# Filler matmuls and tile-by-tile waits on TensorE in the edge loop of the last layer of a four-layer graph network

## What is computed

```python
def _L3_gnn_ref(x, edge_index, W, b):
    loops = jnp.arange(N)
    src = jnp.concatenate([edge_index[0], loops])
    dst = jnp.concatenate([edge_index[1], loops])
    deg = jax.ops.segment_sum(jnp.ones_like(dst), dst, num_segments=N)
    dinv = jax.lax.rsqrt(deg)
    norm = dinv[src] * dinv[dst]
    xw = jnp.matmul(x, W)
    msg = xw[src] * norm[:, None]
    agg = jax.ops.segment_sum(msg, dst, num_segments=N)
    return jax.nn.relu(agg + b)
...
h = jnp.maximum(_layernorm(x), 0.0)
x = x + _L3_gnn_ref(h, edge_index, L3_gnn_W, L3_gnn_b)
return x
```

## Time and profile before

| | us |
|---|---|
| median of 3 runs | 5710.36 |
| lowest and highest | 5703.56, 5723.24 |
| the profiled execution | 5696.5 |
| its span, first to last instruction | 5694.7 |
| mean granted TensorE clock in it | 0.742 |

### The profile page before, as it was taken

The page is one execution under the profiler, slowest core; times in us unless marked ns, Lnnn a source line. Parts: engine busy times, 40 slices in busy tenths (PEclk is TensorE's granted clock), DMA queues, the critical chain, the costliest instruction groups (busy, mean ns, idle before and its releaser), DMA issues. The chain is left out here.

```text
span 5694.7 us, 67915 instructions
## 1 busy us (share of the span) xinstructions
PE 3575.8 (63%) x13714; PEld 2586.3 (45%) x13714; DVE 3362.4 (59%) x9604; ACT 2025.6 (36%) x5849; POOL 3194.3 (56%) x3425
## 2 busy tenths in 40 slices
PE   8666666666699555666656477777777443444444
PEld 5444444444474444544444345555545333333333
DVE  7577777777753556666656456666666443444434
ACT  2455555555463322322222355555655200000000
POOL 1466655555300366666666466666666466666665
PEclk9776777767799777777877667767776676767777
DMA  3343333333310243333333233333333233333332
GB/s 107 90 115 111 110 107 107 107 110 111 91 38 2 84 115 105 106 104 105 104 101 105 60 92 95 96 96 97 96 95 96 63 97 98 97 97 100 96 98 84
DMA packets 345412, 539.66 MB, mean 95 GB/s; under 512 B 75657, under 2 KB 237484, under 8 KB 345036
## 3 DMA queue, kind: packets, MB, share of 16 engines
q0 software_dynamic: 146080, 385.23, 24.4%
q1 hardware_dynamic: 191467, 142.70, 8.9%
q10 hardware_dynamic: 7488, 7.72, 0.4%
HBM read 505.27 MB, written 30.07 MB: 94 GB/s over the span
## 5 line engine op out<-in xcount | busy, mean ns | idle before, releaser
L761 POOL DMA_INDIRECT e_rows<-table,src_idx x2490 | 2356.4, 946 | 1650.5 <-issue 631.3
L853 DVE TENSOR_TENSOR acc<-acc,banks 128x273 f32 (+3 forms) x3320 | 1294.5, 390 | 1392.8 <-DMA prep<-in_prep 555.4
L842 PE MATMUL banks<-e_rows,e_hot 128*128 128x128 f32 (+1 forms) x3320 | 853.2, 409 | 705.7 <-issue 415.5
L842 PEld LDWEIGHTS banks<-e_rows,e_hot 128*128 128x128 f32 x3320 | 704.9, 248 | 847.2 <-issue 692.2
L761 POOL DMA_INDIRECT edge_rows<-table,src_idx x830 | 787.8, 949 | 536.6 <-PE banks L842 210.3
L842 PE MATMUL banks<-edge_rows,e_hot 128*128 128x273 f32 x1660 | 738.7, 577 | 15.2 <-DVE edge_rows L1301 8.2
L842 PE MATMUL banks<-e_rows,e_weighted_hot 128*128 128x257 f32 x1660 | 692.9, 557 | 19.0 <-issue 14.6
L970 ACT ACTIVATE e_apart<-const,dst_loc 128x128 bf16<-128x128 f32 x1664 | 505.7, 388 | 15.9 <-PEq L539 9.1
L842 PEld LDWEIGHTS banks<-e_rows,e_weighted_hot 128*128 128x128 f32 x1660 | 401.0, 269 | 105.2 <-issue 30.5
L842 PEld LDWEIGHTS banks<-edge_rows,e_hot 128*128 128x128 f32 x1660 | 393.9, 269 | 113.2 <-DVE acc L853 15.7
L1583 PE MATMUL banks<-e_wr,e_scaledT 99*128 99x384 f32 (+1 forms) x832 | 278.2, 491 | 105.8 <-ACT e_scaledT L1505 56.1
(11 more groups left out here) (359 smaller groups left out, 5283.5 us busy)
## 6 DMA issues: line engine op xcount, KB each, us to landing
e_edge_in<-in_edge_attr SPq DMA_DIRECT2D x830, 80.0 KB
e_rows<-table,src_idx POOLq DMA_INDIRECT x2490
e_node_rows<-node_line SPq DMA_DIRECT2D x104, 256.0 KB
edge_rows<-table,src_idx POOLq DMA_INDIRECT x830
table<-n_row SPq DMA_DIRECT2D x49, 132.0 KB, 1.7
X<-in_x SPq DMA_DIRECT2D x1, 6272.0 KB
values<-table SPq DMA_DIRECT2D x49, 128.0 KB, 2.0
table<-fn_row ACTq DMA_DIRECT2D x48, 129.0 KB
```

The source lines that it names most:

```text
L761: nc.gpsimd.indirect_dma_start(out=rows[:, u, q, 0:width], out_offset=None, in_=table, in_offset=bass.IndirectOffsetOnAxis(ap=at, axis=0)) ...
L842: ins = nc.tensor.matmul(sums.area(t), onehot, rows, start=True, stop=True)
L853: nc.vector.tensor_tensor(at, at, sums.area(j * G + q), ALU.add).then_inc(added, 1)
```

## The change

It acts in the plain loop alone.

- The gathers of a batch raise 8 semaphores in place of one: `gathered` has `RING * G` = 32 entries there, indexed `u * G + q`, and `tile_arrived(n, q)` gives the count to wait for.
- TensorE no longer waits for all 8 gathers ahead of tile 0. `sum_tile` gets `arrival`, and waits for the one tile's rows right ahead of its matmul. The waits for `hot_ready` (ahead of tile 0) and `added` (ahead of each even tile) stay where they were, and come first.
- Between the wait for `added` and the wait for the rows, TensorE multiplies `ones` (128 x 128) with columns of `const` into the tile's own PSUM area: 512 columns, as two matmuls of 256, ahead of the first tile of a pair, 256 columns, one matmul, ahead of the second. The real matmul, with `start=True`, then overwrites the area. This is 3 filler matmuls for 2 real ones, all of 256 columns.

```diff
@@ gather_batches
-                                                 in_offset=bass.IndirectOffsetOnAxis(ap=at, axis=0)).then_inc(gathered[u], 16)
+                                                 in_offset=bass.IndirectOffsetOnAxis(ap=at, axis=0)).then_inc(gathered[u * G + q if tile_by_tile else u], 16)
 
             turns(gather)
             for u in range(RING):
-                pool.wait_ge(gathered[u], arrived(BATCHES - RING + u, u))
+                if not tile_by_tile:
+                    pool.wait_ge(gathered[u], arrived(BATCHES - RING + u, u))
+                for q in range(G if tile_by_tile else 0):
+                    pool.wait_ge(gathered[u * G + q], tile_arrived(BATCHES - RING + u, q))
...
+        def tile_arrived(n, q):
+
+            return 16 * sum(is_step(m, q) for m in range(n % RING, n + 1, RING))
...
-        def sum_tile(pe, j, q, onehot, rows, summed_tile, added, sums):
+        def sum_tile(pe, j, q, onehot, rows, summed_tile, added, sums, arrival=None):
 
             if not is_step(j, q):
                 return
             t = j * G + q
             if t % sums.group == 0:
                 pe.wait_ge(added, max(0, t - (sums.groups - 1) * sums.group) + 4)
+            filler = sums.filler[t % sums.group] if sums.filler else 0
+            for at in range(0, filler, 256):
+                nc.tensor.matmul(sums.area(t)[:, 0:min(256, filler - at)], ones[:, :], const[:, 0:min(256, filler - at)], start=True, stop=True)
+            if arrival is not None:
+                pe.wait_ge(*arrival)
             ins = nc.tensor.matmul(sums.area(t), onehot, rows, start=True, stop=True)
...
-                gathered = [sem(f"{tag}_gathered{u}") for u in range(RING)]
+                gathered = [sem(f"{tag}_gathered{u}") for u in range(RING if filtered else RING * G)]
...
-                tile_sums = Sums(width, 2, 2, 3) if filtered else Sums(width, 2, 0, 6)
+                tile_sums = Sums(width, 2, 2, 3) if filtered else Sums(width, 2, 0, 6, (512, 256))
...
                             if q == 0:
                                 if filtered:
                                     pe.wait_ge(filtered_rows, j + 1)
-                                else:
-                                    pe.wait_ge(gathered[u], arrived(j, u))
                                 pe.wait_ge(hot_ready, j + 1)
-                            sum_tile(pe, j, q, hot[:, u % 2, q, :], rows[:, u, q, :], summed_tile, added, tile_sums)
+                            arrival = None if filtered else (gathered[u * G + q], tile_arrived(j, q))
+                            sum_tile(pe, j, q, hot[:, u % 2, q, :], rows[:, u, q, :], summed_tile, added, tile_sums, arrival)
```

More of the change, by code:

```diff
@@ L747, in _, with gather_batches @@
                                 cutoff_part(2)
-        def gather_batches(pool, table, width, rows, gathered, summed_tile, sums, picks_read=None):
+        def gather_batches(pool, table, width, rows, gathered, summed_tile, sums, picks_read=None, tile_by_tile=False):
             def gather(n, u):
@@ L811, in build, with __init__ @@
         class Sums:
-            def __init__(self, width, group, first_bank, count):
-                self.width, self.group, self.first_bank = width, group, first_bank
+            def __init__(self, width, group, first_bank, count, filler=()):
+                self.width, self.group, self.first_bank, self.filler = width, group, first_bank, filler
                 self.in_bank = min(group, 512 // width)
@@ L1463, in _ @@
                     def _(pool):
-                        gather_batches(pool, table, width, rows, gathered, summed_tile, tile_sums)
+                        gather_batches(pool, table, width, rows, gathered, summed_tile, tile_sums, tile_by_tile=not filtered)
                     if not filtered:
```

## The result

| | before | after |
|---|---|---|
| median us (20 runs each) | 5694.99 | 5719.63 |
| lowest and highest | 5665.37, 5723.24 | 5692.30, 5746.63 |
| span of the profiled execution | 5694.7 | 5734.4 |
| mean granted TensorE clock in it | 0.742 | 0.783 |

The changed kernel takes 1.005 times as long (95% interval 1.0029 to 1.007), about 25 us more. Its profiled execution, 5736.16 us, lies 16.5 above its median, so the 39.7 us between the two profiled spans are more than the change costs as a rule.

A forecast was written before the change was run, and what follows sets the result against it. GpSimd's 10.0 us a batch plus stalls was taken as the bound. Terms -5 + 22 + 3 = +20 us on the profiled 5696.5 gave about 5716, put at 5730 since the shown median lay 14 above; range 5620 to 5850.

The forecast's parts named there:

- Slower by over 0.3%: Whole kernel: a loss beyond the about 0.3% (17 us) that a measurement can tell from no change; chance 0.48.
- The bound: Last layer's plain loop: GpSimd's 10.0 us of work a batch plus stalls, 150 us over all 830 gathers.
- sums seen late: Last loop's slow stretches: TensorE's sums are noticed late, gathers fill the ring of 32 tiles, then stop some us.
- Step 1: Tile-by-tile waits: nothing in steady state, first batch ends about 5 us sooner; taken as -5 us, between 0 and -10.
- Step 2: Filler at TensorE's restarts lengthens 52 waits: 21 to 133 us if bare, 0 if covered; taken as +22 us.
- Step 3: After the last gather, 14 tiles carry 21 fillers, 8.9 us, beside VectorE's adds; bounds 0 and 9, taken +3 us.
- A: Last loop gains: steady TensorE breaks up long rows of gathers; at best all 150 us of stalls go, 5560; chance 0.25.
- B: Last loop: all filler hidden, GpSimd's waits for sums stay covered; 5700 to 5727 us; chance 0.15.
- C: Last loop: every TensorE restart is at 1.2 GHz, 3.8 us each; +148 us, 5860; chance 0.16.
- D: Last loop: filler doesn't keep the clock, TensorE is the bound below mean 0.75; at worst +585 us, 6295; chance 0.04.
- The signs foretold: Last loop: clock above 0.9, rows of some 20 gathers at 1.25 us, SyncE's stores 0.7 us, pace 1.43 to 1.50 us.

The follow-up runs named there:

- e2: The kernel before plus the filler, still with one wait for all 8 gathers of a batch: ratio 1.0054 to the kernel before, gathers 1196.4 us.
- e12: The kernel before without the last loop's one-hots, matmuls and adds, block work after the last gather: gathers 1132.8 us, whole kernel 1.0348 times as long.
- e1: The changed kernel without filler, waits by tile kept: ratio 1.0005 to the kernel before, gathers 1176.9 us.
- e3: The changed kernel with the one-hot wait moved behind the first pair's filler: ratio 1.0055 to the kernel before, gathers 1195.7 us.
- e5: The changed kernel with each filler matmul of 256 columns cut into two of 128: ratio 1.0107 to the kernel before, gathers 1216.3 us.
- e7: The kernel before with GpSimd only 16 tiles ahead of the sums in the last loop, not 32: ratio 0.9988, gathers 1176.5 us.
- e11: The changed kernel without filler, waits by tile kept, GpSimd at most 16 tiles ahead: ratio 0.9974 to the kernel before, gathers 1186.7 us.
- e6: The changed kernel with 5 filler matmuls of 256 columns for a pair, not three: ratio 1.0191 to the kernel before, gathers 1244.2 us.
- e8: The kernel before with GpSimd only 24 tiles ahead of the sums in the last loop, not 32: ratio 0.9999, gathers 1177.0 us.
- e10: The kernel before with the last loop gathering rows of 512 bytes in place of 1 KB: ratio 0.9981, gathers 1182.1 us.
- e9: The kernel before plus 4980 one-column copies on idle ScalarE in the last loop: ratio 1.0286, gathers 1198.2 us, tail 176.4 us.
- e4: The changed kernel with one filler matmul of 256 columns a pair, not three: ratio 1.0016 to the kernel before, gathers 1182.9 us.

## Why the prediction came out right, and where its steps were wrong

**The number.** +20 us was forecast and +25 measured; 5730 was forecast and 5719.63 measured, since over 20 runs the kernel before came to 5694.99 and not 5710.36. "Slower by over 0.3%" had the largest chance of the three. The terms as the runs show them are 0, about 20 and 9, which is 29 (31 by the medians in e2). The sum stood up, but the reason given for it did not: two terms were off in opposite directions, and the largest was right by luck.

**The bound: failed.** It said 10.0 us a batch of GpSimd's own work plus 150 us of stalls, as if the stalls were an accident of the turns. e12 shows that gathers alone, past the first 190, take 1.40 us each when they follow one another. The kernel before has 1181.3 us and e12 1132.8. Of the difference, 18.2 us lie behind the 200th gather (899.5 for 881.3), which is 5.5 ns for each of the 5.3 instructions of the other engines that go with a gather; the other 30.3 lie within the first 200 (281.8 for 251.5). By this account GpSimd runs ahead of the limit in the stretches at 1.25 us, and the slow stretches pay it back: with only gathers there the payment is even, with other engines at work it is made in stops of GpSimd and in the steps of 0.7 and 1.4 us seen on TensorE and ScalarE. It would explain what I read as "sums seen late" in the earlier trace rows, though no run shows VectorE's late add itself to be such a step.

**Step 1, waits by tile: 0 for the forecast -5.** The start goes as worked out, with the first sum 8 us earlier in the loop, but the first 100 gathers take 143.8 us and took 141.5 (e1, without filler: 140.9). An early sum can't help where gathers are the bound and the ring is still empty. The step went wrong by counting the first batch's delay as time on the path, against its own statement that GpSimd is the bound. e1 confirms 0 (1.0005).

**Step 2, the filler: +22 forecast, about 20 measured, by another mechanism.** 4980 added records at 4.0 ns are 20 us between first and last gather. The forecast had put the time on restarts, 52 waits lengthened behind the one-hot, and had then taken a sixth of the upper bound. e3 removed that wait and the cost stayed; e5 doubled the instructions at the same TensorE time and the cost doubled. A sixth of 133 was a choice, and that it met the number is luck. The step's arithmetic on TensorE itself held: 8.5 us a batch hid beside GpSimd's pace, at 0.94 where above 0.9 was foretold.

**Step 3, the tail: +9.0 for +3, at the upper bound given.** The forecast counted the 14 tiles of the last two batches. In the changed kernel TensorE still has 13 to 14 pairs to do after the last gather, at 2.15 us a pair, from 5697.90 to 5727.17 = 29.3 us. Before, VectorE set the end with 1.26 us a pair and its one-hots. The step also cut the backlog before too short: at the last gather, 5667.18, TensorE was still in the batch ahead of those 28 records, so it had some 20 tiles left and not 14 (an estimate from this row of TensorE's timeline):

```profile
5665.40 5.38 PE L842 MATMUL banks<-e_rows,e_hot 128*128 128x256 f32 x16 [2.29 <-issue]
```

A pair with filler is slower than VectorE's two adds, so nothing covers it there. The ring's lead of up to 32 tiles was known, and the step should have used it; e7 and e11, with half the lead, show tails of 17.0 and 14.7.

**The rivals.** A's mechanism took place without its gain: the rows of gathers fell from 13.4 to 6.8 and TensorE ran at 0.94. But broken rows saved nothing, here or in e5 (6.1 gathers to a row, and the slowest pace of the runs that GpSimd bounds), and the 150 us that A hoped for are mostly the 0.15 us by which 1.40 exceeds 1.25. B (all hidden) holds the absolute time, 5719.63, but only because its base was 15 us too high; as a difference, from -10 to +17 us, it lies below the 25 measured, and e2 shows that the filler isn't hidden. C needs ends of waits on TensorE longer by 100 us; they went from 57.3 to 76.6. D's condition did not arise; TensorE is the bound in e6, at 56 records a batch, and not yet at 40. The signs foretold were right for the clock and for the pace (1.459 in 1.43 to 1.50), wrong for rows of some 20 gathers, and half wrong for SyncE's stores (0.54 us at the median for 0.69).

**The clock.** The Trainium skill ("TensorE: Matmul & The Clock Gate", section "Why this matters for your kernels") advises against idle gaps between bursts. On the clock the traces agree: 0.70 to 0.72 in the last loop without filler, 0.76 with a third of it, 0.93 to 1.00 with all or more. The time didn't follow: TensorE was busy 413 of 960 us in e1, and its faster matmuls brought no gather forward.

**What stays open.** What the shared thing is, and whether it is one thing; that is inferred from the way the charges add up. The runs show that it is charged by gathers and instructions, and not by bytes or by TensorE's time, and that a filler matmul or a copy, which raises no semaphore, is charged as well. What it is in the chip they don't tell. One rival is untested: every execution here has the span and the granted clock of its core on record, so no run shows the loop without a record being taken of it, and the recording of instructions may itself be part of the charge. The head start doesn't fit yet either. With e12's 28 us to draw on, the kernel before should run at 1.25 us for its first 150 gathers or so (28 / 0.18, an estimate from e12 and its own later pace of 1.430), but it has lost 16.5 us by the 100th, e7 and e8 as much. The changed kernel's trace, at 1.463 us a gather behind the 200th, lies above the line as well (1.447 in e2). The kernel before was profiled on its own, and its gathers' 1181.3 us lie 4 to 5 above those of e1, e7 and e8 (1176.5 to 1177.0, on two chips); e10 and e11 on a third have 1182.1 and 1186.7. Differences of some 5 us between single traces therefore prove nothing, and neither the 5.5 ns nor the 4 to 7 of e9 is exact.

## What to carry to other kernels

Before you put filler on an engine, ask whether anyone waits for that engine's speed: here the clock rose from 0.71 to 0.94 and the kernel lost 0.5%, because the loop hung on its gathers and the filler's instructions had a price of their own. When the engine that seems to be the bound shows stalls that move but don't shrink as you change the turns, run that engine's work alone: it showed that the price of a gather was 1.40 us and not the 1.25 that stands in most rows. What is left to try in such a loop is fewer gathers, fewer instructions and a shorter backlog at its end; of these only the last was run here, and its gain, 9 to 11 us of tail, is within what the whole kernel's times can tell.

## What the hardware showed that I had not expected

- A gather of 128 rows takes 1.25 us for the first 190 or so in a row and 1.40 us from then on, with no other engine at work (e12). In the whole loop the pace is the same at 512 bytes a row as at 1 KB (e10: 671 gathers for 672 in 960 us).
- While gathers go out back to back, instructions of other engines, even ones that wait for nothing, come at times in steps of 0.7 or 1.4 us: filler matmuls in the changed kernel (1.46 and 1.40 us apart), ScalarE's copies in e9 (260 in 100 us for 1074).
- Held to 1.50 us a gather by TensorE, this is gone: SyncE's store takes 12 ns at the median in place of 691 (e6).
- An added TensorE record costs 4 ns of such a loop whether it has 256 columns or 128 (e2, e4, e5), and a copy on idle ScalarE perhaps 4 to 7 ns (e9).
